# Projections and scores of attention from upper and lower parts in scaled 16-bit floats instead of rounded 32-bit ones

## The reference

```python
qkv = (x @ w_qkv.T).reshape(B, S, 3 * H, D)     # x is the layer-normed input
q, k, v = qkv[:, :, :H], qkv[:, :, H:2 * H], qkv[:, :, 2 * H:]
logits = jnp.einsum('bqhd,bkhd->bhqk', q, k) * scale
weights = jax.nn.softmax(logits, axis=-1)
combined = jnp.einsum('bhqk,bkhd->bqhd', weights, v).reshape(B, S, H * D)
return combined @ w_out.T
```

## Time and profile before

| | us |
|---|---|
| median of 3 runs (lowest, highest) | 927.24 (923.82, 927.65) |
| the profiled execution | 927.37 |
| its span, first to last instruction | 925.6 |

### The profile page before, as it was taken

How to read it: one execution, slowest core, us unless ns; L and a number is a source line. 1 busy time by engine, 2 the same in 40 slices (tenths; PEclk the granted TensorE clock), 3 DMA queues, 4 the chain that set the end, 5 groups by cost and what they waited for, 6 DMA issues and landing times.

```text
span 925.6 us, 12929 instructions
## 1 busy us (share of the span) xinstructions
PE 838.9 (91%) x4314; PEld 580.2 (63%) x4314; DVE 767.4 (83%) x1573; ACT 584.0 (63%) x978; POOL 413.6 (45%) x423
## 2 busy tenths in 40 slices
PE   4889989999999999999999998679787999998997
PEld 2666766776676666666667665457554555554686
DVE  3789999899989999999999998585599687876637
ACT  4668657766778567667667667364545767657531
POOL 2114335344445257777777771171323434443301
PEclk9999999999999999999999999899989999999999
DMA  3497858766877677867867777130000000000001
GB/s 111 76 191 148 156 109 180 159 131 120 200 147 140 134 136 140 153 128 145 168 108 139 134 135 143 33 106 1 1 1 0 1 1 1 2 1 1 1 1 46
DMA packets 276867, 86.29 MB, mean 93 GB/s; under 512 B 267584, under 2 KB 272448, under 8 KB 276416
## 3 DMA queue, kind: packets, MB, share of 16 engines
q1 hardware_dynamic: 275520, 80.05, 44.6%
q0 software_dynamic: 992, 5.34, 2.0%
q10 hardware_dynamic: 288, 0.07, 0.0%
HBM read 17.29 MB, written 1.05 MB: 20 GB/s over the span
## 4 chain that ended last, share of the span: by engine, by line
PE 50%; DVE 29%; issue 8%; ACT 8%; DMA 3%; POOL 1%; SPq 0%; POOLq 0%; DVEq 0%; ACTq 0%
PE ps L1061 11%; PE ps L1062 10%; PE ps L1063 10%; DVE nmax L1683 6%; DVE EP L1698 5%; PE ps L1084 4%; PE ps L1314 3%; PE ps L1099 3%; PE ps L1300 3%; DVE ps L1868 3%; PE ps L1279 2%; DVE ptm L1782 2%; DVE st L1602 1%; ACT EP L1464 1%; DMA ET<-EP 1%
## 5 line engine op out<-in xcount | busy, mean ns | idle before, releaser
L1464 ACT ACTIVATE EP<-ps,rinv 128x1024 f16<-128x1024 f32 x128 | 142.7, 1115 | 53.0 <-DVE rinv L1693 52.1
L1698 DVE SCALAR_TENSOR_TENSOR EP<-ps,rinv,EP 128x1024 f16<-128x1024 f32 x128 | 163.6, 1279 | 5.5 <-ACT EP L1464 4.9
L1454 ACT ACTIVATE ps<-ps,nmax 128x1024 f32<-128x1024 f32 x128 | 139.5, 1090 | 32.2 <-DVE nmax L1683 31.2
L1683 DVE TENSOR_REDUCE nmax<-ps 128x1 f32<-128x1024 f32 x128 | 154.9, 1210 | 2.0 <-PE ps L1063 1.8
L2009 POOL TENSOR_TENSOR wgu<-wgu,ptm 128x688 f32<-128x688 f32 x60 | 100.6, 1677 | 42.9 <-DVE ptm L1782 40.2
L1061 PE MATMUL ps<-ET,VH 128*128 128x512 f16 x256 | 98.2, 384 | 20.8 <-DMA ET<-EP 14.2
L1061 PE MATMUL ps<-KH,QH 128*128 128x512 f32 x256 | 107.2, 419 | 8.8 <-DVE KL L1665 5.1
L2009 POOL TENSOR_TENSOR wdn<-wdn,ptm 128x512 f32<-128x512 f32 x45 | 58.5, 1301 | 95.9 <-DVE ptm L1782 94.4
L1063 PE MATMUL ps<-KH,QL 128*128 128x512 f32 x256 | 100.8, 394 | 0.0
L1062 PE MATMUL ps<-KL,QH 128*128 128x512 f32 x256 | 100.7, 393 | 0.0
L1063 PE MATMUL ps<-ET,VL 128*128 128x512 f16 x256 | 97.8, 382 | 0.0
(11 more groups left out here) (239 smaller groups left out, 2153.1 us busy)
## 6 DMA issues: line engine op xcount, KB each, us to landing
wqr<-in_wqk SPq DMA_DIRECT2D x16, 256.0 KB, 3.6
wgu<-in_tern POOLq DMA_DIRECT2D x3, 1024.0 KB, 6.2
wvr<-in_wv SPq DMA_DIRECT2D x8, 256.0 KB, 4.3
wor<-in_wo SPq DMA_DIRECT2D x16, 128.0 KB, 3.1
ET<-EP SPq DMA_TRANSPOSE x128, 4.4
X<-in_x SPq DMA_DIRECT2D x2, 512.0 KB, 6.0
prw<-in_down_idx POOLq DMA_DIRECT2D x2, 256.0 KB, 6.1
tern<-in_l_wuq_rep SPq DMA_DIRECT2D x1, 512.0 KB, 4.9
```

The source lines that it names most:

```text
L1454: e.activation(bank, bank, ACT.Exp, bias=nmax[:, c:c + 1], scale=1.0, accum_out=rsum[:, c:c + 1]).then_inc(exped.sem, 1)
L1464: e.mul(EP[:, n % NE_RING, 0, :], SB(u, j), rinv[:, c:c + 1]).then_inc(e_hi.sem, 1)
L1683: e.tensor_reduce(nmax[:, c:c + 1], SB(u, j), AX.X, ALU.max, negate=True).then_inc(maxed.sem, 1)
L1698: e.scalar_tensor_tensor(out=EP[:, n % NE_RING, 1, :], in0=SB(u, j), scalar=rinv[:, c:c + 1], in1=EP[:, n % NE_RING, 0, :], op0=ALU.mult, ...
```

## The change

The parts of x, Q, K and of the weights of Q, K and V become 16-bit floats in tiles of their own (`xh`, `xl`, `qh`, `ql`, `kh`, `kl`); the output projection and all later stages keep theirs. Line numbers below are those of the changed kernel where they differ.

x is scaled up by a constant 2^11 when it is split. The weights of Q and K of a pair of heads get one power of two for each of the four 128-column pieces: ACT squares each piece and sums it along the row, PE sums over partitions, DVE makes the powers of two and the product of those of Q and K (`s_unit`), POOL multiplies both heads' weights. The scale of the logits is no longer put into Q: `exp` takes it as its `scale`, and ACT first multiplies the row maximum by it. The raw weights of Q and K have two buffers instead of one, and are loaded two heads ahead.

The pieces of the diff below are in this order: tiles, PE, ACT (three pieces), DVE, POOL; their `norm_wqk` is one step on three engines.

```diff
-            wqr = sbuf(ctx, "wqr", [P, 2, 256])
-            wqh, wql = (sbuf(ctx, n, [P, 2, 2, 256], F32R) for n in ("wqh", "wql"))
+            wqr = sbuf(ctx, "wqr", [P, 2, 2, 256])
+            wqh, wql = (sbuf(ctx, n, [P, 2, 2, 256], F16) for n in ("wqh", "wql"))
...
-                        mm = three(SB(u, j)[:, cs], QH[:, b, qs], QL[:, b, qs], KH[:, b, cs], KL[:, b, cs], True, True)
+                        mm = three(SB(u, j)[:, cs], qh[:, b, qs], ql[:, b, qs], kh[:, b, cs], kl[:, b, cs], True, True)
                     mm.then_inc(scored.sem, 1)
+                elif what == "norm_wqk":
+                    h, = at
+                    i, freed = BANK[step]
+                    w.each([freed])
+                    w.wait_ge(*ones_in[0])
+                    w.wait_ge(*q_squared[h, 3])
+                    e.matmul(ps[:, WB + i, 0:4], f32(ones[:, :]), wsum[:, :], start=True,
+                             stop=True).then_inc(q_normed.sem, 1)
...
+                elif what == "square_wqk":
+                    h, = at
...
+                    for i in range(4):
+                        w.wait_ge(*wqk_in[i // 2][h + i // 2])
+                        if i > 0:
+                            w.wait_ge(*q_squared[h, i - 1])
+                        e.activation(wsq[:, :, :], wqr[:, i // 2, :, i % 2 * P:i % 2 * P + P], ACT.Square,
+                                     accum_out=wsum[:, i:i + 1]).then_inc(q_squared.sem, 1)
...
-                    e.mul((QH, KH)[which][:, h % 2, cs], bank, (SCALE0, 1.0)[which]).then_inc(qkv_hi.sem, 1)
+                    e.mul((qh, kh)[which][:, h % 2, cs], bank, 1.0 / X_UP).then_inc(qkv_hi.sem, 1)
...
-                    e.activation(bank, bank, ACT.Exp, bias=nmax[:, c:c + 1], scale=1.0,
+                    e.mul(nms[:, c:c + 1], nmax[:, c:c + 1], s_unit[:, h4:h4 + 1]).then_inc(max_down.sem, 1)
+                    w.wait_ge(*max_down[u, j])
+                    e.activation(bank, bank, ACT.Exp, bias=nms[:, c:c + 1], scale=s_unit[:, h4:h4 + 1],
...
+                elif what == "norm_wqk":
+                    h, = at
+                    w.wait_ge(*q_normed[h])
...
+                    e.tensor_scalar(wnorm[:, :], ps[:, WB + BANK[step][0], 0:4], 2.0 ** -100, None,
+                                    ALU.max).then_inc(q_norm.sem, 1)
+                    w.wait_ge(*q_norm[h])
+                    e.tensor_scalar(wpow[:, :].bitcast(I32), wnorm[:, :].bitcast(I32), 24, 23, ALU.logical_shift_right,
+                                    ALU.logical_shift_left).then_inc(q_power.sem, 1)
+                    w.wait_ge(*q_power[h])
...
+                    e.tensor_scalar(wfac[:, :].bitcast(I32), wpow[:, :].bitcast(I32), -1.0, float(201 << 23), ALU.mult,
+                                    ALU.add).then_inc(q_factor.sem, 1)
...
+                    e.scalar_tensor_tensor(out=s_unit[:, h % 4:h % 4 + 2], in0=wpow[:, 0:4:2], scalar=SCALE0 * 2.0 ** 106,
+                                           in1=wpow[:, 1:4:2], op0=ALU.mult, op1=ALU.mult).then_inc(s_scale.sem, 1)
...
+                elif what == "norm_wqk":
+                    h, = at
+                    w.wait_ge(*q_factor[h])
+                    w.wait_ge(*q_squared[h, 3])
+                    for i in range(2):
+                        factors = wfac[:, 2 * i:2 * i + 2].rearrange("p (k w n) -> p k w n", k=1, n=1)
+                        weights = wqr[:, i, :, :].rearrange("p k (w n) -> p k w n", w=2)
+                        e.tensor_tensor(weights, weights, factors.broadcast_to([P, 2, 2, P]),
+                                        ALU.mult).then_inc(q_scaled.sem, 1)
```

The order is rewritten. In the ramp, squaring and scaling stand ahead of the first projection; within a unit the first projection's parts, exp, row_inv and some slots change places, PE's own list stays the same but for the new small matmul:

```diff
-    before = ("t0 t1 n0 n1 n2 n3 n4 k0 T0 v0 n5 n6 n7 X0 x0 y0 T1 X1 y1 X2 y2 x1 k1 x2 x3 v1 v2 S0 X3 M0 e0 y3 "
-             "S1 x4 e1 v3 h0 v4 X4 e2 x5 M1 y4 S2 i0 l0 M2 i1 h1 i2 M3 X5 S3 y5 l1 x6 l2 X6 h2 x7 X7 e3 y6 y7").split()
+    before = ("t0 t1 n0 n1 n2 n3 n4 k0 T0 K0 Q0 v0 n5 n6 n7 X0 x0 y0 T1 X1 y1 X2 y2 x1 Q1 x2 x3 v1 v2 S0 X3 M0 "
+             "e0 y3 S1 x4 e1 v3 h0 v4 X4 e2 x5 M1 y4 S2 i0 l0 M2 i1 h1 i2 M3 X5 S3 y5 l1 x6 l2 X6 h2 x7 X7 e3 "
+             "y6 y7").split()
...
-    order = ("i3 f0 F0 A7 M0 p0 S0 h3 l3 e0 X0 O0 x0 S1 i0 o0 h0 y0 S2 x1 X1 l0 e1 M1 p1 w0 S3 w1 y1 p2 h1 i1 "
-             "M2 e2 p4 A0 A1 l1 i2 X2 M3 y2 A2 x2 A3 A4 A5 A6 l2 w2 p3 h2 e3").split()
+    order = ("i3 f0 F0 A7 M0 S0 h3 p0 e0 l3 X0 x0 o0 i0 h0 e1 O0 y0 x1 S1 M1 l0 S2 X1 p1 w0 w1 p4 S3 i1 y1 A0 "
+             "A1 X2 A2 M2 p2 l1 i2 M3 y2 h1 e2 x2 A3 A4 A5 A6 h2 l2 w2 p3 e3").split()
```

More of the change, by code:

```diff
@@ L391, in build @@
         ident = sbuf(top, "ident", [P, P])
+        with ExitStack() as ctx:
+            qh, ql, kh, kl, xh, xl = (sbuf(ctx, n, [P, 2, 1024], F16) for n in ("qh", "ql", "kh", "kl", "xh", "xl"))
         QH, QL, KH, KL = (sbuf(top, n, [P, 2, 1024], F32R) for n in ("QH", "QL", "KH", "KL"))
@@ L499, in build @@
         x_in = [landing(f"x_in{i}") for i in range(2)]
-        wqk_in, wv_in, wo_in, raw_in = (landing(n) for n in ("wqk_in", "wv_in", "wo_in", "raw_in"))
+        wv_in, wo_in, raw_in = (landing(n) for n in ("wv_in", "wo_in", "raw_in"))
+        wqk_in = [landing(f"wqk_in{i}") for i in range(2)]
         index_in = [landing(f"index_in{i}") for i in range(2)]
@@ L517, in build @@
         ones_in, v_squared, v_scaled = (signal(n, "POOL") for n in ("ones_in", "v_squared", "v_scaled"))
+        q_squared, max_down, q_normed, q_scaled = (
+            signal(n, by) for n, by in (("q_squared", "ACT"), ("max_down", "ACT"), ("q_normed", "PE"), ("q_scaled", "POOL")))
+        q_norm, q_power, q_factor, s_scale = (signal(n, "DVE") for n in ("q_norm", "q_power", "q_factor", "s_scale"))
         v_normed, norm_turned = signal("v_normed", "PE"), signal("norm_turned", "PE")
@@ L643, in build @@
         lut_in.mark(0)
-        wqk_in.mark(0)
+        wqk_in[0].mark(0)
+        wqk_in[1].mark(1)
         wv_in.mark(0)
@@ L1017, in _ @@
                 e.dma_start(X[:, 4 * i:4 * i + 4, :], x_v[:, 4 * i:4 * i + 4, :]).then_inc(x_in[i].sem, 16)
-            e.dma_start(wqr[:, :, :], a["wqk"][:, 0, :, :]).then_inc(wqk_in.sem, 16)
+            for h in range(2):
+                e.dma_start(wqr[:, h, :, :], a["wqk"][:, h, :, :]).then_inc(wqk_in[h].sem, 16)
             e.dma_start(wvr[:, :, :], a["wv"][:, 0, :, :]).then_inc(wv_in.sem, 16)
@@ L1127, in _ @@
                         for k in range(2):
-                            mm = three(bank[:, i * 256:i * 256 + 256], XH[:, k, ts], XL[:, k, ts],
+                            mm = three(bank[:, i * 256:i * 256 + 256], xh[:, k, ts], xl[:, k, ts],
                                        wvh[:, k, :], wvl[:, k, :], k == 0, k == 1)
@@ L1664, in _ @@
                         w.wait_ge(*scored[unit_of(h - 2, (half, 1)[which]), 3])
-                    e.scalar_tensor_tensor(out=lo[:, h % 2, cs], in0=bank, scalar=(SCALE0, 1.0)[which],
-                                           in1=f32(hi[:, h % 2, cs]), op0=ALU.mult,
+                    e.scalar_tensor_tensor(out=lo[:, h % 2, cs], in0=bank, scalar=1.0 / X_UP,
+                                           in1=hi[:, h % 2, cs], op0=ALU.mult,
                                            op1=ALU.subtract).then_inc(qkv_lo.sem, 1)
```

80 lines of the change are left out of this document (61 added, 19 removed).

## The result

The changed kernel takes 939.97 us (median of 4 runs, 937.38 to 940.72), the one before 926.79 us in the same job (4 runs). The ratio is 1.0143, with a 95% interval of 1.0113 to 1.0173: **slower by 1.4%**, some 13 us. The profiled execution took 939.58 us, its span is 937.8 us, the granted clock 0.985.

The account below looks back on a forecast made before the run. In the heads stage PE led, with DVE near its limit in later groups. Terms -5.6 - 1.0 + 1.5 + 1.5 + 2.2 + 6.3 = +4.9 us, and -1 us for the list, gave 931.3 us (median 931.1); range 918 to 942 us.

Parts of the forecast that it names:

- The rate of the matmuls: PE, scores and projections: 512-column steps fall from 230.6 to 216.5 ns, V gains 0 to 3.8 us, together 20 us.
- The rival of a rate that belongs to the pattern: Scores and projections: 16-bit operands also step at 230 ns, so 6.6 us of gain is lost, 938 us; chance 0.05.
- What of it counts: Heads stage: only PE time on the chain pays, 9.6 us at most; 5.6 early, 1.3 later, 1 in the ramp.
- The start: Ramp: squares, factor and POOL's scaling delay the first projection from 15.17 to about 21.5 us, costing 6.3 us.
- the rival in which 4 of the 6 us come back: Ramp: DMAs and bank waits give back 4 of the start's 6 us, 927 us; chance 0.18.
- Squares: ACT, between exp and `cast_e`: four squares, 2.4 us a pair, cost nothing unless DVE is not late.
- POOL: Weight scaling on POOL, 20 us in all, is hidden; holding DVE up costs 1.5 us.
- The measuring step: DVE and PE, each pair: 0.7 us of small operations, 0.4 us wait; 1.5 us early, later offset by recovered waits.
- The new order: Rearranged unit list: freer for exp, nothing changed on PE; gains 1 us, between 0 and 4.
- The multiplication: ACT, ahead of each of 128 exps: 0.27 us, counting 8 times in ramp and stage end, 2.2 us; nothing within groups.
- DVE becomes the bound and is held up: Heads stage: 18 us more on DVE, half on the path, PE's clock falling at times, about 941 us; chance 0.15.
- the early ones shorter by 2 us: Sign of being right: early groups of the heads stage, where DVE has slack, shorten by 2 us.

Follow-up runs that it names:

- type alone, old order: Changed kernel without squares, measuring, weight scaling and multiplication before exp, with the earlier ramp and unit order: 918.2 us, 0.9906 of the kernel before.
- start only: Changed kernel without the multiplication before exp; squares, measuring step and POOL's multiplications remain for the first pair of heads only: 929.82 us, 1.0036 of the kernel before.
- type alone in the new order: Changed kernel without squares, measuring, weight scaling and multiplication before exp, earlier ramp, new unit order kept: 922.29 us, 0.9960 of the kernel before.

## Why the prediction was right and where it was wrong

The time, 940 us, lies in the range and on the side that had the highest chance, but 9 us above the forecast and outside its own 928 to 934. That it lies within 918 to 942 is luck in part: the upper end came from a rival in which POOL holds DVE up, not from the terms that were missed, and those were off by up to 6 us each in both directions. Taken one after the other, the runs give this, in us of the kernel before:

| Part | Predicted | Measured | From |
|---|---|---|---|
| 16-bit parts alone | -11.0 | -8.7 | type alone, old order |
| New order of a unit | -1.0 | +5.0 | new less old order, type alone |
| Start | +6.3 | +7.0 | start only less type alone |
| POOL's multiplications | +1.5 | -2.3, not to be told from 0 | two runs |
| Measuring step, 7 pairs | +5.2 | +8.0 | with less without |
| Squares | 0 | -1.6, not to be told from 0 | with less without |
| Multiplication before exp | +2.2 | +5.8 | changed less without |
| Sum | +3.2 | +13.2 | |

(The prediction set 3.4 x 1.3 = 4.4 us of gain in later groups against 3.7 of DVE work in the measuring step and wrote nothing for both; here they are in their rows, so its sum stands 0.7 us lower. The measured column must add up, since each row starts where the last one ends.)

- *The rate of the matmuls*: right. Eighteen matmuls of scores and projections start within 368.31 and 371.99 us, 17 steps of 216.5 ns. The 256-column products of V, whose gain I had put at 0 to 3.8 us, got it:

```profile
368.31 0.39 PE L1094 MATMUL ps<-kh,qh 128*128 128x512 f16 x1
...
371.99 0.38 PE L1096 MATMUL ps<-xh,wql 128*128 128x512 f16 x1
...
339.70 0.28 PE L1094 MATMUL ps<-wvh,xh 128*128 128x256 f16 x1 [0.31 <-DVE VL L1738]
...
340.91 0.27 PE L1096 MATMUL ps<-wvh,xl 128*128 128x256 f16 x1
```

  Eleven steps in 1.21 us are 110 ns. The Trainium skill's rule (TensorE: Matmul & The Clock Gate, Back-to-back issue gap) gives 256 / 2.4 + 2.5 = 109 ns: it holds for 16 bits at both widths, and not for fp32r, which stepped at 230.6 and 118. The section calls this the gap of an isolated matmul and gives about 131 ns for 512 columns in a stream in which each has its weight load; the streams here, which are of that kind, step at 216.5 ns. The rival of a rate that belongs to the pattern is out.
- *What of it counts*: right. Of some 20 us of PE time 8.7 arrive once everything else is left as it was.
- *The start*: right in kind and size. PE began at 20.32 us and not 21.5: the factor was there 0.5 us sooner, since the squares began at 12.31 and ended at 14.49 us and not at 15.06, and POOL's multiplications took 1.02 us each, not 1.27, another 0.5. The run with the start alone pays 7.0 us, give or take 3.6, for 5.7 us of delay; the rival in which 4 of the 6 us come back is out.
- *Squares*: right for the new order. *POOL*: its multiplications cost nothing that could be told from 0. The contention itself is there, though: a `ptm` that starts inside an operation of POOL is longer, as shown above, and in the run in which POOL's multiplications remain and the measuring step is out, four start inside a multiplication and take 1.17 to 1.36 us. In the changed kernel none does, yet the 77 `ptm` from 60 to 586 us take 57.9 us together, in the kernel before 54.6, and in the type alone in the new order 54.9. So "DVE's table operations longer than now", which I had named as a sign of being wrong, came out, by 6%, and what is left of it in the time is too small to be measured.
- *The measuring step*: the price was right, 1.11 us, but on average it is paid by all 7 pairs, 8.0 us, give or take 3.6, where 5.2 were charged. The step that failed is most likely "In three early groups I charge 0.5 us each to the PE path", as if DVE's slack of the early stretches covered its side; no run takes the step out of the early groups alone.
- *The new order*, the largest miss. I took "freer for exp and changes nothing on PE" from the list and priced only what it frees. It costs 5.0 us, give or take 3.2. The likely place is the score banks, for which PE waits 14.6 us instead of 2.5. The list shows `l0` behind `M1`, where it had stood ahead of it; I never asked who waits for `rest_e`.
- *The multiplication*: "within the groups I charge nothing" fits the new order by itself (2.9 us, give or take 3.3, against 2.2); beside the other additions it was 5.8, give or take 4. Its own length was mis-sized: 0.27 us taken, 0.42 measured, because the row of 0.20 us that I took it from the earlier trace rows is the read-out of a sum, not a multiplication by a column, and the column as exp's scale was not priced.
- *The rival that came closest* is "DVE becomes the bound and is held up", at 941 us. Its outcome came, DVE did become the bound, and its 1.1 us for each pair is the measured one. It named "DVE's operations on the small tiles take over 0.5 us each" as the point from which it decides; they took 0.17. DVE became the bound for another reason: the faster matmuls alone do it, as the chain of the type alone shows (51.0% to 25.7%), and the order, the measuring step and the multiplication are then added to an engine that already leads. Its other half hardly came: the granted clock was about the same (0.985 against 0.989), and what POOL added to DVE can't be told in the time.

Of the signs that I named, the rate came out and PE's idle time is ended by DVE. The groups of the second half are longer than the 69 to 70 us that I gave (from `vp` to `vp` 70.6 and 71.9 us from 337 us on, before 69.3 and 69.8), and "the early ones shorter by 2 us" failed: the three from 123 to 337 us have 71.9, 71.1 and 71.0 us, before 72.7, 70.4 and 70.2. There PE is free of work for longer and gains little by it.

## What to carry over

When a change comes with a new order of work, price the order by itself, in both directions: for each operation that moves back, who waits for what it frees. A cost on a chain with little slack is not proportional: exp was late 6 times, 0.42 us more made it late 40 times, and the same addition cost 2.9 or 18.5 us depending on the list. And once an engine is made faster, look again at who leads the chain before pricing what the change adds elsewhere: here DVE led it already. A scale folded into an operand that is written once for each head was cheaper than one applied to each tile of scores, by 5.8 us, give or take 4.

## What was not expected of the hardware

- A 128x1 ACT operation with a column as factor takes 294 ns, where one without took 202; a column as exp's scale adds 87 ns to 1090.
- POOL's multiplication of 128x512 by a broadcast factor took 1.02 us each at the start and 1.17 on average in the groups, less than its subtraction of the same size before (1.27 to 1.29).
- The same DVE operation, `ptm` of 128x688, took 0.57 us, and 1.82 us when it started inside an operation of POOL.
